# Four residual layers on one core: x1 and x2 kept transposed, with layer 0's second half moved ahead of unit 0

## The reference

```
x = x + (w0[a].T @ x + bias0[a][:, None])                   # layer 0: mixes the 64 positions of a sample
x = x + lora(h, Wd, Ad[a], Bd[a]),  h = silu(lora(x, Wg, Ag[a], Bg[a])) * lora(x, Wu, Au[a], Bu[a])
                                                            # layer 1: 512 -> 2048 -> 512; lora(x, W, A, B) = x@W + (x@A)@B, rank 16
x = x + x @ W2.T + scal2[b] * ((x @ A2[b].T) @ B2[b].T)     # layer 2
x = x + w3[c].T @ x                                         # layer 3: mixes positions again
```

## Time and profile before

| | |
|---|---|
| median of 3 runs | 765.71 us (765.18 to 767.59) |
| the profiled execution | 767.69 us, span 765.9 us, 10652 instructions |
| granted TensorE clock, mean | 0.99 |
| PE busy | 727.8 us, 95% of the span |
| DVE, ACT, POOL busy | 601.1, 284.8 and 255.3 us |
| HBM traffic | 56.94 MB read, 8.39 MB written, 85 GB/s |

### The profile page before, as it was taken

How to read it: one execution, slowest core, us unless ns; L and a number is a source line. 1 busy time by engine, 2 the same in 40 slices (tenths; PEclk the granted TensorE clock), 3 DMA queues, 4 the chain that set the end, 5 groups by cost and what they waited for, 6 DMA issues and landing times.

```text
span 765.9 us, 10652 instructions
## 1 busy us (share of the span) xinstructions
PE 727.8 (95%) x3626; PEld 606.9 (79%) x3626; DVE 601.1 (78%) x1010; ACT 284.8 (37%) x508; POOL 255.3 (33%) x489
## 2 busy tenths in 40 slices
PE   6779889999999999989899999999999999899997
PEld 4547678888888888878778888888888888788886
DVE  7975768797878778799898979787888877766675
ACT  3445523333424333434353334242434333134232
POOL 4724231515223232350327162534425231241100
PEclk9979999999999999999999999999999999999999
DMA  7366520313212121203723232221212061212112
GB/s 209 87 81 194 164 80 29 104 37 108 83 56 83 55 84 56 83 27 111 248 59 109 71 103 73 70 86 58 89 55 85 28 192 32 79 29 70 42 55 83
DMA packets 65941, 66.02 MB, mean 86 GB/s; under 512 B 31712, under 2 KB 48096, under 8 KB 65888
## 3 DMA queue, kind: packets, MB, share of 16 engines
q1 hardware_dynamic: 57248, 45.92, 19.9%
q0 software_dynamic: 7296, 19.41, 8.7%
q10 hardware_dynamic: 1344, 0.02, 0.1%
HBM read 56.94 MB, written 8.39 MB: 85 GB/s over the span
## 4 chain that ended last, share of the span: by engine, by line
PE 84%; DVE 10%; issue 2%; ACT 2%; DMA 1%; POOLq 0%; POOL 0%; ACTq 0%; DVEq 0%
PE bank L1376 36%; PE bank L1474 22%; PE bank L1384 7%; PE bank L1633 6%; PE bank L1483 4%; PE bank L1622 2%; PE bank L1326 1%; PE bank L1599 1%; PE bank L1639 1%; DVE XC L882 1%; PE bank L1650 1%; PE bank L1611 1%; DVE hid L1001 1%; PE bank L1353 1%; DVE hs L1007 1%
## 5 line engine op out<-in xcount | busy, mean ns | idle before, releaser
L1376 PE MATMUL bank<-XC,WC 128*128 128x512 f32 x1344 | 332.9, 394 | 6.7 <-DVE tmp L975 2.2
L1376 PEld LDWEIGHTS bank<-XC,WC 128*128 128x128 f32 x1344 | 245.5, 190 | 54.8 <-issue 4.7
L1474 PE MATMUL bank<-wds,hs 128*128 128x512 f32 x768 | 187.6, 394 | 6.6 <-DVE X L1017 3.3
L1474 PEld LDWEIGHTS bank<-wds,hs 128*128 128x128 f32 x768 | 142.9, 190 | 35.8 <-DVE wds L960 3.8
L398 POOL DMA_INDIRECT BR<-in_L_cond_Bu_dram,boffs x64 | 71.9, 1124 | 265.7 <-DVE BL L954 251.1
L398 POOL DMA_INDIRECT BR<-in_L_cond_Bg_dram,boffs x64 | 76.1, 1189 | 95.2 <-DVE BL L954 80.2
L620 ACT ACTIVATE hs<-hid 128x512 fp32r<-128x512 f32 x64 | 40.3, 630 | 164.4 <-DVE hid L1001 111.4
L1017 DVE TENSOR_TENSOR X<-bank,X 128x512 f32<-128x512 f32 x128 | 86.5, 686 | 17.5 <-PE bank L1474 15.3
L614 ACT ACTIVATE hid<-hid 128x512 f32<-128x512 f32 x48 | 30.4, 633 | 148.4 <-DVE hid L984 75.9
L1384 PEld LDWEIGHTS bank<-UT,BL 128*128 128x128 f32 x512 | 76.4, 190 | 10.0 <-issue 2.1
L1384 PE MATMUL bank<-UT,BL 128*128 128x256 f32 x512 | 81.9, 283 | 1.3 <-ACT hid L611 1.3
(11 more groups left out here) (152 smaller groups left out, 827.9 us busy)
## 6 DMA issues: line engine op xcount, KB each, us to landing
RW<-in_L_cond_Wg_dram SPq DMA_DIRECT2D x16, 512.0 KB, 4.4
RW<-in_L_cond_Wu_dram SPq DMA_DIRECT2D x16, 512.0 KB, 5.1
RD<-in_L_cond_Wd_dram SPq DMA_DIRECT2D x16, 512.0 KB, 3.5
out_dram<-XR SPq DMA_DIRECT2D x16, 256.0 KB, 2.0
X<-in_x_dram SPq DMA_DIRECT2D x8, 256.0 KB, 6.2
udp<-in_x_dram SPq DMA_DIRECT2D x8, 256.0 KB, 4.5
x1park<-RD SPq DMA_DIRECT2D x8, 256.0 KB, 4.2
x2park<-X SPq DMA_DIRECT2D x8, 256.0 KB, 2.5
```

The source lines that it names most:

```text
L1376: last = nc.tensor.matmul(psum[:, :], WC[:, t, left, a, k, :], XC[:, right, b, k, :], start=(first and k == 0 and n == 0), stop=(k == 1 an ...
L1474: last = nc.tensor.matmul(psD[j % 2][:, :], hs[:, f, a, j * P:(j + 1) * P], wds[:, f, b, :], start=(f == 0 and n == 0), stop=(f == 1 and n ...
```

## The change

x1 and x2 are kept with features on the partitions from layer 0 on.

- Layer 0 uses the x rows as the stationary operand and the weight as the moving one, four 128x128 fp32 matmuls a pair, so the result lands transposed in PSUM. GpSimd adds the identity while it places each weight block (a two-input add in place of a copy). For half 0 DVE adds a bias tile (`xr_sum`); the tile is made by two matmuls of a 40-row table against ones. For half 1 the bias is one more matmul of the pair. All first-layer transposes go, and x1_sum, add_identity and x1_bias with them.
- Half 1 of layer 0 moves ahead of unit 0: two pairs after each of the first steps of the adapters' inputs, four more around p5 of unit 0. Four x buffers (two of them in RD) are used for it.
- Features are in natural order: Wg, Wu are loaded as `(k p)`, and the adapter tables Ag, Au in rows of 16 floats (64 bytes) in place of 64 floats (256 bytes).
- POOL places all 16 pairs' weights before its first gather; ACT, DVE and SP have their prologues reordered. The Wd load of unit 0 waits only for layer 0's last matmul.
- Down is computed transposed (Wd block stationary, hidden activations moving), same counts and sizes.
- In the last stage there are no transposes of x2. `lora_down` gives x2 transposed: 12 matmuls of 256 columns a duo in place of 6 of 512. The identity is added to W2 and w3 once (`w2_identity`, `w3_identity` on DVE), so `x3_sum` and `y_sum` go: ACT and DVE split the PSUM of layer 2 directly, and ACT copies the output (`y_out`).

The core of the diff:

```diff
 def layer0(p):
     pe.wait_ge(s_w0c, p + 1)
...
-    nc.tensor.matmul(psD[p % 2][:, :], w0bd_of(p), x_of(p), start=True, stop=True).then_inc(s_l0, 1)
+    if p >= 4:
+        pe.wait_ge(s_xr, p - 3)
+    for k in range(KT):
+        last = nc.tensor.matmul(l0_bank(p)[:, k * P:(k + 1) * P], by_feature(x_of(p))[:, k, :], w0bd_of(p),
+                                start=(k == 0), stop=(p < HP and k == KT - 1), skip_group_check=True)
+    if p < HP:
+        last.then_inc(s_l0, 1)
+        return
+    if p == HP:
+        pe.wait_ge(s_bias, 2)
+    nc.tensor.matmul(l0_bank(p)[:, :].rearrange("p (k t) -> p k t", k=KT), ones[0:BROWS, :],
+                     bsel[:, p * P:(p + 1) * P].unsqueeze(1).to_broadcast([BROWS, KT, P]),
+                     start=False, stop=True, skip_group_check=True).then_inc(s_l0, 1)
...
 # PE's order
-warm(5)
-layer0(0)
-pe.wait_ge(s_ident, 1)
-for p in range(1, HP):
+warm(24)
+biases_to_all()
+warm(4)
+for p in range(HP):
     layer0(p)
-    transposes(p - 1)
-transposes(HP - 1)
...
 adapters_in(0, 0)
+layer0(HP)
+layer0(HP + 1)
 adapters_in(0, 1)
+layer0(HP + 2)
+layer0(HP + 3)
 select(0, 0)
...
 # inside unit 0: p6, select 1, layer0(HP + 4), selects 2 and 3, layer0(HP + 5), p5, then
+if unit == 0:
+    layer0(HP + 6)
+    layer0(HP + 7)
...
 # POOL
-last = nc.gpsimd.tensor_copy(w0bd_of(p)[rows, rows].rearrange("p (c f) -> p c f", f=KT),
-                             w0tab[rows, bass.ds(cols[half], RANK), :])
+last = nc.gpsimd.tensor_tensor(w0bd_of(p)[rows, rows].rearrange("p (c f) -> p c f", f=KT),
+                               w0tab[rows, bass.ds(cols[half], RANK), :],
+                               ident[rows, rows].rearrange("p (c f) -> p c f", f=KT), ALU.add)
...
 for q in range(HQ):
     select_a(0, q, cols)
-pool.wait_ge(s_boffs, 1)
-gather_b(0)
 for g in range(2, 4):
     late = adapters(8 * g, 8)
     for p in range(4 * g, 4 * g + 4):
         place_w0(p, late[2 * (p - 4 * g):2 * (p - 4 * g) + 2])
+pool.wait_ge(s_boffs, 1)
 pool.wait_ge(s_w0c, PAIRS)
+gather_b(0)
 gather_b(1)
...
 # SP
-     a.rearrange("n (p k) r -> p n (k r)", k=KT)).then_inc(s_al, 16)
+     a.rearrange("n (k p) r -> p (n k) r", p=P)).then_inc(s_al, 16)
...
 # the last stage on PE
 for d in range(DUOS):
-    if d + 1 < DUOS:
-        transposes2(d + 1)
-    layer2(d, 0)
-    lora_out(d, 0)
...
+    for q in range(2):
+        layer2(d, q)
+        lora_out(d, q)
     if d + 1 < DUOS:
         lora_in2(d + 1)
+    if d + 2 < DUOS:
+        lora_down(d + 2)
     if d >= 1:
+        layer3(d - 1, 0)
         layer3(d - 1, 1)
...
 # layer2(d, q) now waits for the split of the duo before, not for x3_sum
-    pe.wait_ge(c_x3, 2 * d + q - 1)
+    pe.wait_ge(c_x3l, 2 * (d - 1) + q + 1)
```

More of the change, by code:

```diff
@@ L437, in _ @@
                 cols = []
-                for g in range(2):
-                    cols += adapters(8 * g, 8)
-                    for p in range(4 * g, 4 * g + 4):
+                for n, count in ((0, 4), (4, 6), (10, 6)):
+                    cols += adapters(n, count)
+                    for p in range(n // 2, (n + count) // 2):
                         place_w0(p, cols[2 * p:2 * p + 2])
@@ L1106, in up_window @@
                         t1_sum(1)
+                    if unit == ALL - 2:
+                        w3_identity(0)
+                        w3_identity(1)
+                    if unit == ALL - 1:
+                        w2_identity()
                 def evicts(unit, quads, which):
@@ L1308, in warm @@
                 def warm(times):
-                    pe.wait_ge(s_nothing, 1)
+                    pe.wait_ge(s_ones, 1)
                     for _ in range(times):
-                        nc.tensor.matmul(psE[:, 0:QT], nothing[:, 0:P], nothing[:, :], start=True, stop=True)
-                    for _ in range(times):
-                        nc.tensor.matmul(psE[:, 0:P], nothing[:, 0:P], nothing[:, 0:P], start=True, stop=True)
+                        nc.tensor.matmul(psE[:, 0:P], ones[:, :], ones[:, :], start=True, stop=True)
                 def layer0(p):
```

593 lines of the change are left out of this document (273 added, 320 removed).

## The result

The changed kernel takes 757.12 us (median of 8 runs, 754.15 to 762.56); the kernel before took 766.21 beside it (8 runs, 765.18 to 768.01). The ratio is 0.989, interval 0.986 to 0.992: faster, by 9 us, and not by the 21 that were forecast; 757.1 lies above the range (738 to 753.5). The profiled execution took 756.74 us, span 754.9, so 1.8 around it as before. The forecast for the span was 744.9: **10.0 us are missing.**

What follows compares the result with a forecast made beforehand. PE was taken as the bound, busy 95% of the span; -10.8 (to unit 1), -2.3 (unit 1) and -7.9 (last stage) sum to -21.0 against a 765.9 us span, giving 744.9, so 744.7 us, ratio 0.973; range 738 to 753.5.

Steps and rivals of the forecast that it cites:

- p5 held by the gather at 46.8: Prologue: the first gather, behind all GpSimd weight placing, cancels the earlier x1; p5 of unit 0 stays at about 46.8 us.
- The side remark on GpSimd's contention: Prologue: without SBUF contention with VectorE, GpSimd's copies would take 0.23 us each and the sum 3 to 4 us less.
- Second-half pairs 8 to 13 (7.1 us) are hidden in PE's idle time: Prologue: these layer 0 pairs, moved ahead of unit 0, cost nothing; without that cover they would cost 7.1 us.
- VectorE's order in the prologue: Prologue: bias tables and w3's zeros added, add_identity and longer x1_sum removed, about nothing in sum for DVE.
- From p5 to unit 1: Unit 0: c11's adapters at 52.4 us, unit 1 starting at 72.4 instead of 83.2, -10.8 us.
- Two waits ... come from ACT and DVE held up by the Wd load: Unit 1: waits of 1.28 and 1.03 us vanish because Wd is issued at about 50 us, -2.3 us.
- What is late next in the unit is DVE's eviction, as it is today; I give that nothing: Unit 1: after the Wd waits go, DVE's eviction is late as before; priced at nothing.
- Middle and turn: Middle units and turn: transposed down has equal count and columns, table and x1 loads hide behind PE; 0 us.
- Last stage: Last stage: transposes -7.0, two waits -2.5, lora_down +0.5, w2_identity +0.8, end +0.3; -7.9 us, duo 11.06 us.
- Adds cost twice a copy: Rival, prologue: GpSimd's 16 adds take 18.3 us for 12.3, p5 6 later, low PE clock; 752.8 us, chance 0.18.
- The prologue is not held by POOL: Rival, prologue: POOL ends by 35 us, p5 follows DVE's order at 43.2 at full clock; 740.6 us, chance 0.22.

Runs made afterwards that it cites:

- e2: Changed kernel with layer 0's pairs 8 to 15 and their ScalarE copies back inside unit 0, their x loads following: 760.96 us, ratio 0.992.
- e1: Changed kernel with 32 filler matmuls (8, 8 and 16) in PE's prologue pauses ahead of adapters_in(0, 0): 760.22 us, ratio 0.990.
- e12: Changed kernel with prologue reordered on VectorE, ScalarE and PE, x1 parking behind unit 1's Wd load, unit 1's third U sum earlier: 753.15 us, ratio 0.982.
- e14: e12 with GpSimd copying layer 0's weights in place of adding the identity: 753.44 us, ratio 0.983.
- e13: e12 with the first gather issued between GpSimd's adds for pairs 8 to 11 and those for 12 to 15: 753.26 us, ratio 0.983.
- e6: Changed kernel with only VectorE's prologue order changed: move matrices and masks in idle time, first A tiles ahead of W's sums: 760.61 us, ratio 0.993.
- e5: Changed kernel with the eight parking transfers of x1's second half issued behind unit 1's Wd load: 759.69 us, ratio 0.991.
- e9: Changed kernel with VectorE's third U sum ahead of the low parts of Wd, Ad and Wu, in unit 1 alone: 755.45 us, ratio 0.984.
- e11: Changed kernel with eight unused identity transposes put back into each duo of the last stage: 765.19 us, ratio 0.998.
- e4: Changed kernel with GpSimd copying layer 0's weights in place of adding the identity: 760.79 us, one run.

## Why the prediction was wrong, step by step

**p5 held by the gather at 46.8: the step that failed.** "So the gather eats what the earlier x1 gives, and p5 stays where it is" took the slowest chain to be GpSimd's. GpSimd itself kept the forecast: `select_a` ended at 27.0 us (26.5 forecast), the late adds took 12.2 us (12.3) and ended at 39.5 (39). In the profile after:

```profile
27.66 11.83 POOL L409 TENSOR_TENSOR w0second<-adsel,ident 64x64 f32<-64x64 f32 x15
40.42 1.15 POOL L421 DMA_INDIRECT BR<-in_L_cond_Bg_dram,boffs  x1 [0.93 <-POOL w0second L409]
41.88 1.78 POOL L421 DMA_INDIRECT BR<-in_L_cond_Bg_dram,boffs  x1 [0.30 <-issue]
```

But ScalarE and PE take their instructions in order, and the moved pairs stand in both queues in front of the chain. ScalarE after:

```profile
44.80 0.60 ACT L536 ACTIVATE XB<-bank 128x512 f32<-128x512 f32 x1 [0.92 <-PE bank L1354]
45.29 1.05 ACT L550 ACTIVATE XC<-hid 128x1024 fp32r<-128x1024 f32 x1
...
48.63 0.60 ACT L536 ACTIVATE XB<-bank 128x512 f32<-128x512 f32 x1 [2.29 <-PE bank L1354]
49.37 1.06 ACT L550 ACTIVATE XC<-hid 128x1024 fp32r<-128x1024 f32 x1
50.33 0.61 ACT L597 ACTIVATE BL<-BR 128x512 fp32r<-128x512 f32 x1
```

And VectorE after:

```profile
41.62 1.22 DVE L941 TENSOR_TENSOR hid<-XA,hid 128x1024 f32<-128x1024 f32 x1
...
46.38 1.23 DVE L916 TENSOR_TENSOR XC<-hid,XC 128x1024 fp32r<-128x1024 f32 x1 [2.94 <-issue]
...
48.12 1.22 DVE L936 TENSOR_TENSOR hid<-XA,hid 128x1024 f32<-128x1024 f32 x1
```

VectorE has the sum T1 ready at 42.84, but ScalarE copies its high part only at 45.29, behind the copies of pairs 10 and 11, for which it waits on PE: 2.45 us. VectorE's low part of T1 follows at 46.38 and its next sum, T4, ends at 49.34; ScalarE copies T4's high part at 49.37 and splits B at 50.33. The split shows no wait for the gather, and `u_own`, and so p5, stand behind it. (The copy of pair 12, with its wait of 2.29 us for PE, ends no later than T4's sum, so it is not the one releaser.)

e2, with the pairs back, has p5 3.0 us earlier, or 3.4 counted from the first layer 0 matmul. Since the gather binds in e2 and was issued 1.1 us later there, an estimate from these numbers is 4.1 us for the pairs' place; the other 2.1 of the 6.2 would then be the gather's own lateness (issued 1.1 us later than forecast, its second part slow to issue). The low clock on `adapters_in` (2.3 us, see e1) and the late start of layer 0, at 10.26 for 7.90, are in the chain ahead of all this and are not further terms of the sum. What stays open: why the weight table landed late in 11 of 14 traces of kernels with the change (first matmul at 9.98 to 10.70 us, and at 8.43 to 8.66 in the other three), while both traces of the old form have 7.9.

The side remark on GpSimd's contention, "without it the copies would take 0.23 each and the sum 3 to 4 us less", is too low by its own rows: 16 copies in 9.2 us of busy time against 16 at 0.23, 3.7, is 5.5 less. Nothing in the forecast hangs on it.

**"Second-half pairs 8 to 13 (7.1 us) are hidden in PE's idle time": wrong, and the larger lesson.** PE was idle 3.5 us of 40 to 50 us before, but in pieces that end where VectorE releases the next select or p5. A pair is also dearer than the 1.18 us priced: each of the eight instructions is 0.12 to 0.14, as estimated, but with the bias matmul the pair is 1.46 us. The estimate was for one late pair 0.95 + 0.23; it measured about 1.0 + 0.45, so the 40x512 bias matmul is the mis-sized price here: 0.23 us for about 0.44. e2 against the changed kernel gives 3.8 to 4.15 us of unit 1's start for the whole move. How much order could mend is seen in e12 to e14: unit 1 is 67.0 to 67.7 us behind the first layer 0 matmul there. With that and the start at 7.90 as before, unit 1 would begin at about 75, still 2.5 us above the forecast 72.4, and PE's 10 us windows from 40 to 80 us in e12 are 9.12, 8.35, 10.00 and 9.69 busy. So of the 7.3 us missing at unit 1's start 2.4 are the late table and some 2 are order. The rest, some 2.9, no run takes apart: in it are PE work for which there was no idle time, the 1.5 us of low clock on e12's second `adapters_in` and the 1.3 that e13's earlier gather gives from p5 on.

**VectorE's order in the prologue** was passed over with "about nothing in sum". The sum is right, the place is not: VectorE is idle from 8.4 to 12.4 us and then has 9.66 us of work between 20 and 30 (in e1's window), and its last part is what `adapters_in` waits 4.10 us for. e6 moved that by 2.8 us.

**From p5 to unit 1.** The 5.6 us to c11 are right, the 1.17 us of waiting for `p1_copy` included (1.3 forecast). The rest is 1.0 longer, of which e5 measures 0.8 as the parking transfers beside the gather. The prediction had them in SP's queue and looked only at who needs Wu.

**Unit 1: "Two waits ... come from ACT and DVE held up by the Wd load", -2.3: the step that failed in the second place.** Wd was there early this time; the wait of 1.28 fell to 0.38, and that of 1.03 grew to 2.54. VectorE after:

```profile
82.46 0.68 DVE L1031 TENSOR_TENSOR tmp<-bank,tmp 128x512 f32<-128x512 f32 x1
...
85.92 1.28 DVE L999 TENSOR_TENSOR wds<-RD,wds 128x512 fp32r<-128x512 f32 x2
...
90.40 0.68 DVE L1004 TENSOR_TENSOR ads<-adsel,ads 128x512 fp32r<-128x512 f32 x1
91.00 0.68 DVE L1014 TENSOR_TENSOR tmp<-bank,tmp 128x512 f32<-128x512 f32 x1
```

Nothing in it waits; it is one queue from 80.6 to 91.7 us, and the sum that frees PE is at its end. e9 shows that its order alone removes the wait and 2.9 us of the gate half. What the prediction read in the trace of before was largely right: there ScalarE waited 1.47 us for Wd, and VectorE paused 0.61 us for the split of Wd and 0.27 for ScalarE's copy ahead of the same sum (at 93.05), which explains up to 0.9 of the 1.03. What failed is "What is late next in the unit is DVE's eviction, as it is today; I give that nothing": without a pause VectorE's queue was still too long. Why unit 1 took longer than before, not only as long, was not tested alone: at its start VectorE was 2.8 us behind with the sum of unit 0's c12 (82.46 for 79.68), while before it was level (83.12 for 83.20).

**Middle and turn** are right to 0.3 us, the down product with exchanged operands included.

**Last stage** is right: -8.6 for -7.9, the duo at 11.06, `w2_identity` seen as a wait of 1.06 us on Wd's split where 0.26 stood before (+0.8). e11 shows the size of a transpose group, 0.88.

**The rivals.** "Adds cost twice a copy" came nearest with its time, 752.8 for 757.1, but for a wrong reason: the adds took 12.2 us and not 18.3, and e4 says that they are not on the path. "The prologue is not held by POOL" was true, and did not give 740.6: ScalarE, PE and VectorE held it together. No rival had "the moved work stands in front of the chain in an in-order queue", and none had unit 1 longer than before.

## What to carry to other kernels

Work moved into idle time is hidden only if it stands behind, in each engine's program order, everything on the chain: ask of each queue it enters which instruction is now behind it. A wait in the trace names the last releaser; before pricing its removal, read the releasing engine's queue backwards, and if it runs without a pause, the cure is its order and not the input of one of its instructions. And when one wait is mended, the next queue takes over, so order changes are to be tried together (e6 alone gained nothing, e12 with the same edit is, with e13, the fastest).
